# Second norm's rows and routed tiles' rows turned by transposing transfers, with a new written order

## The reference, cut to what matters

```python
# x: (8, 1024, 256)
h = layernorm(x) * (1 + ca) + sa
x = x + ga * attention(h)               # 16 heads, causal softmax
h = layernorm(x) * (1 + cb) + sb        # the second norm
shared = silu(h @ w1.T) * (h @ w2.T) @ w3.T          # hidden 1024
scores = sigmoid(h @ router_w.T)                     # 8 experts, the 2 best of scores + bias
routed = sum over the two chosen e of scores[e] * (silu(h @ a_e.T) * (h @ b_e.T)) @ w3_e.T
x = x + gb * (shared + routed)
```

## Time and profile before

| what | value |
|---|---|
| three timed runs | 2047.53, 2051.80, 2051.96 us; median 2051.8 us |
| the profiled execution, its own time | 2070.19 us |
| its span | 2068.4 us |
| granted TensorE clock, mean | 0.954 of full speed |
| batches 2 to 6 ("loop") | 199 us each, 422 to 1418 us of the span |
| "end" | from about 1594 us to 2068.4 us, 474 us |

### The profile page before, as it was taken

How to read it: one execution, slowest core, us unless ns; L and a number is a source line. 1 busy time by engine, 2 the same in 40 slices (tenths; PEclk the granted TensorE clock), 3 DMA queues, 4 the chain that set the end, 5 groups by cost and what they waited for, 6 DMA issues and landing times.

```text
span 2068.4 us, 48010 instructions
## 1 busy us (share of the span) xinstructions
PE 1855.7 (90%) x17942; PEld 1081.0 (52%) x17942; DVE 1589.9 (77%) x4447; ACT 1078.7 (52%) x1417; POOL 820.1 (40%) x825
## 2 busy tenths in 40 slices
PE   5688899998999899989998998999988998999884
PEld 2233445453545454545454544555444886888663
DVE  7998989888888888888888887988972565665573
ACT  1566646654665565556555565565545354444321
POOL 1021243424333333332343234323333377776452
PEclk7789999999999999999999999999999999999997
DMA  4347321102111111111111212021214366876794
GB/s 133 118 150 216 107 68 38 48 19 77 48 38 43 52 48 38 48 48 48 38 56 40 56 36 72 22 66 30 58 36 156 78 113 125 163 140 107 193 291 138
DMA packets 109664, 175.69 MB, mean 85 GB/s; under 512 B 14576, under 2 KB 80376, under 8 KB 108288
## 3 DMA queue, kind: packets, MB, share of 16 engines
q1 hardware_dynamic: 82656, 136.37, 22.0%
q0 software_dynamic: 26592, 36.00, 9.5%
q10 hardware_dynamic: 192, 0.26, 0.1%
HBM read 76.43 MB, written 70.44 MB: 71 GB/s over the span
## 4 chain that ended last, share of the span: by engine, by line
PE 58%; DVE 16%; DMA 8%; SPq 5%; ACT 5%; issue 4%; POOL 3%; another core or an unknown queue 1%; ACTq 0%; DVEq 0%; POOLq 0%
PE pair L1831 13%; PE pair L1816 10%; PE pair L1770 6%; PE pair L1794 6%; PE pair L1863 5%; PE pair L1883 5%; DVE pair L1264 4%; PE pair L1744 3%; ACT arena L1061 3%; DVE max_part L1258 2%; PE pair L1910 2%; PE pair L1874 2%; SPq L656 2%; DMA v_sb<-sum 2%; SPq L657 2%
## 5 line engine op out<-in xcount | busy, mean ns | idle before, releaser
L1061 ACT ACTIVATE arena<-pair 128x1024 f32<-128x1024 f32 (+1 forms) x640 | 574.9, 938 | 295.8 <-PE pair L1794 286.5
L1264 DVE CUSTOM_DVE_ANT_0 pair<-pair,mask 128x512 f32<-128x512 f32 (+3 forms) x1024 | 472.1, 520 | 51.6 <-PE pair L1770 48.5
L1831 PE MATMUL pair<-feat_parts,ffn_sb 128*128 128x512 f16 x1536 | 393.1, 391 | 3.6 <-ACT arena L1061 2.4
L875 POOL TENSOR_SCALAR_AFFINE_SELECT arena<-arena 128x512 f32<-128x512 f32 x256 | 163.5, 650 | 560.7 <-ACT arena L1061 560.1
L1816 PE MATMUL pair<-arena,v_sb 128*32 128x256 f32 (+1 forms) x5120 | 320.7, 369 | 6.7 <-issue 3.9
L1258 DVE TENSOR_REDUCE max_part<-pair 128x2 f32<-128x1024 f32 x256 | 312.5, 1221 | 14.3 <-PE pair L1770 10.9
L938 POOL DMA_INDIRECT sum<-arena,feat x142 | 229.8, 1618 | 103.4 <-DVE arena L1490 49.2
L1770 PE MATMUL pair<-arena 48*128 48x512 f16 (+3 forms) x1536 | 213.2, 341 | 54.9 <-ACT arena L1061 19.1
L944 POOL TENSOR_TENSOR hidden<-silu_h,hidden 128x512 f16<-128x512 f32 x128 | 152.2, 1193 | 238.1 <-ACT hidden L1094 237.8
L1794 PE MATMUL pair<-arena 50*128 50x256 f16 (+1 forms) x2560 | 215.4, 265 | 21.8 <-ACT arena L1061 6.2
L1831 PEld LDWEIGHTS pair<-feat_parts,ffn_sb 128*128 128x128 f16 x1536 | 136.5, 100 | 170.6 <-issue 47.0
(11 more groups left out here) (211 smaller groups left out, 2345.2 us busy)
## 6 DMA issues: line engine op xcount, KB each, us to landing
arena<-parts SPq DMA_DIRECT2D x380, 64.0 KB, 2.3
feat<-lists SPq DMA_DIRECT2D x71, 265.0 KB
sum<-feat_parts SPq DMA_DIRECT2D x9, 1024.0 KB, 8.3
rows<-x SPq DMA_DIRECT2D x8, 1024.0 KB, 5.5
x_sb<-x SPq DMA_DIRECT2D x16, 512.0 KB, 4.9
sum<-norm SPq DMA_DIRECT2D x14, 512.0 KB, 4.2
ffn_parts<-hidden SPq DMA_DIRECT2D x8, 768.0 KB, 4.4
arena<-ffn_parts SPq DMA_DIRECT2D x8, 768.0 KB, 7.4
```

The costliest lines, as they stand in the source:

```text
L875: gp.affine_select(p, p, [[0, GH], [1, P]], ALU.is_ge, 0.0, 0, -1).then_inc(masked, 1)
L1061: sc.activation(to[:, :, lo:QC], of[:, :, lo:QC], ACT.Exp, scale=SCALE / QK_SCALE ** 2).then_inc(exp_done, 1)
L1264: last = vec.tensor_tensor_reduce(scored, scored, mask[:, 512 - nk:], scale=1.0, scalar=NEG, op0=ALU.add, op1=ALU.max, accum_out=max_part[ ...
L1831: last = mm(to[:, 0:512], w_up[s][W_PART[i]][:, f, m * RH + h * P:m * RH + (h + 1) * P], feat_parts[:, A_PART[i], f, c * 512:(c + 1) * 512 ...
```

## The change

PE no longer turns the second norm's rows or the tiles' rows, and ACT and DVE no longer copy them. SP issues transposing transfers that write feat_parts and tile_feat directly. The steps `low:h` and PSUM banks for `ln` and `xr` are gone. tile_feat has four buffers in place of two. A tile now takes two transfers: a transposing one of 256 rows x 512 values from the list in memory, and a plain one of the last 9 f32 of each row. For a half of the second norm there are 4 transposing transfers, each of 128 rows x 512 values, SBUF to SBUF. All six lists and their banks are written anew.

```diff
+            def turn_rows(f, v, h):
+                sp.wait_ge(row_low, at_half(f, h))
+                if v == "second" and h == 0:
+                    sp.wait_ge(zeroed, ZEROED)
+                if past(f):
+                    sp.wait_ge(up_full, at_up(f - 1, 8 * h + 7))
+                    sp.wait_ge(router_full, at_half(f - 1, h))
+                for t in range(4 * h, 4 * h + 4):
+                    sp.dma_start_transpose(feat_parts[:, :, :, t * P:(t + 1) * P].rearrange("p a f n -> p (a f) n"),
+                                           rows16[:, t, 0:2 * D]).then_inc(feat_in[h], 16)
...
                 if i >= 2:
-                    sp.wait_ge(tile_turned, at_tile(i - 2))
                     sp.wait_ge(id_ready, at_tile(i - 2))
+                if i >= 4:
+                    sp.wait_ge(tile_full, at_tile(i - 4))
...
-                sp.dma_start(tile_rows[i % 2], list_rows(row)).then_inc(rows_in[i % 2], 16)
+                sp.dma_start_transpose(tile_feat[i % 4].rearrange("p a f n -> p (a f) n"),
+                                       list16[bass.ds(row, ROWS), 0:2 * D]).then_inc(tile_in_turn[i % 4], 16)
+                sp.dma_start(tile_rows[i % 2][:, :, D:], list_rows(row)[:, :, D:]).then_inc(rows_in[i % 2], 16)
...
-            def take_rows(i, of):
-                act.wait_ge(tile_turned, at_tile(i))
-                sc.activation(tile_feat[i % 2].rearrange("p a f n -> p (a f n)"), of[:, 0:4 * ROWS], ACT.Copy).then_inc(tile_taken, 1)
...
-            def feature_low(f, v, h):
...
-            def tile_turn(i, to):
...
             def tile_up(i, to):
-                pe.wait_ge(tile_taken, at_tile(i))
+                pe.wait_ge(tile_in_turn[i % 4], (i // 4 + 1) * 16)
...
                     elif kind == "router":
-                        pe.wait_ge(feat_high, at_half(f, h))
-                        pe.wait_ge(feat_low, at_half(f, h))
+                        pe.wait_ge(feat_in[h], (f + 1) * TURNED)
```

More of the change, by code:

```diff
@@ L126 @@
[L126 to L147, removed]
+        scores:4 scores:5 max:1:7 max:1:8 max:1:9 scores:6 values:0 values:1 values:2 share:0 share:1 raw:0 qk:2 turn_out:0 normalise:0 max:1:10 values:3
@@ L153 @@
[L153 to L164, removed]
@@ new lines @@
+        scores:14 values:10 values:11 halves:0 values:12 values:13 shifts:1 max_turn:1 scores:15 scores:16 max:2:0 values:14 values:15
+        scores:17 raw:2 max:2:1 values:16 ln:0 scores:18 max:2:2 turn_out:1 scores:19 normalise:1 scores:20 turn_out:2 normalise:2 max:2:3 values:17 values:18
+        scores:21 max:2:4 scores:22 router:0 up:0:0 up:0:1 load_x:1 route:0 scores:23 scores:24 up:0:2 values:19 up:0:3 raw:3 max:2:5 up:0:4 up:0:5
+        scores:25 scores:26 scores:27 rank:0 place:0 turn_out:3 normalise:3 values:20 values:21 max:2:6 raw:4 scatter:0 scatter:1 max:2:7
@@ L191 @@
-        scores:18 down:-2:0 down:-2:1 down:-2:2 max:2:0 scores:19 ln:0 low:0 down:-1:0 max:2:1 max:2:2 values:16 values:17 router:0 values:18 route:0
-        values:19 raw:3 scores:20 scores:21 up:0:0 up:0:1 turn_out:2 normalise:2 up:0:2 up:0:3 up:0:4 max:2:3
-        scores:22 up:0:5 turn_out:3 normalise:3 down:-1:1 down:-1:2 scores:23 max:2:4 max:2:5 rank:0 place:0 hid:0 values:20 values:21 raw:4 up:1:0
-        scores:24 up:1:1 up:1:2 up:1:3 up:1:4 up:1:5 scores:25 max:2:6 max:2:7 values:22 values:23 scatter:0
@@ L323 @@
 WORK["start"] += [("max", 0, p) for p in range(MAXES)] + [("max_turn", 0)]
-DOUBLE = ("scores", "max", "op", "ot", "ln", "turn", "qk", "v", "mods", "tup")
-SINGLE = ("down", "router", "max_turn", "rank", "count", "xr", "ty")
+DOUBLE = ("scores", "max", "op", "ot", "turn", "qk", "v", "mods", "tup")
+SINGLE = ("down", "router", "max_turn", "rank", "count", "ty")
 BANKS = 8
@@ L620, in adaln_layer @@
         SHIFTED = 16 * 2
+        TURNED = 16 * 4
         PADS_OUT = 16 * (NE + 1)
```

337 lines of the change are left out of this document (168 added, 169 removed).

## The result

The changed kernel takes 1963.49 us (median of 4 runs, 1959.63 to 1969.33) against 2049.66 us (2043.60 to 2051.96, 4 runs) for the kernel before: ratio 0.9586, 95% interval 0.9553 to 0.9619, 86 us less. The profiled execution took 1963.7 us, its span is 1961.8 us.

The account below looks back on a forecast made before the run. PE was taken to bound both the loop batches and "end"; 21 (tiles) + 12.6 (norm) + 22 (hole) - 3 ("second") = 53 us off the 2051.8 us median gave about 2000 us, range 1975 to 2070 us.

Parts of the forecast that it names:

- Part 1: Tiles: removing PE's turns, 71 x 0.45 = 32 us at full price, counted as 21 us saved.
- Part 3: Loop batches: new list moves load_x1 ahead, shrinking the hole at the x load; 22 us saved over five batches.
- the lists carried at nothing: All stages: the rest of the new lists, not priceable from the old trace, so no term in the sum.
- Part 2: Second norm: removing PE's turns of its rows saves 1.8 us a batch, 12.6 us over seven batches.
- the discounts to 80% and a quarter: Tiles: 53 before 1900 us counted at 80%, 19 us; the 18 behind at a quarter, 2 us.
- Part 4: Transposing transfers: 1.27 us a tile at the low end taken, 5.07 at the high; 17.4 ns per 256 B, issues 0.59 us.
- The 3 us lost in "second": Stage "second": only 3 to 4 us between ln:0 and router:0, so 3 us lost, once.
- Rival (a): New wait at router:0 or scores:20 from slower transfers, PE standing 21 us over seven batches; 2020 to 2025 us, 17%.
- (b): Loop batches: the hole at the x load stays because scatters cannot come earlier; about 2022 us, 12%.
- (c): Transfers become the bound of "end" at 5.07 us a tile, making the kernel slower; about 2190 us, 15%.
- one of its signs: In "end": DMA share of 0.9 or more, with PE waiting for the transposing transfer before a tile's first matmul.
- (d): Everywhere, "first" too: the newly written lists open holes and give the gain back; 2045 to 2060 us, 8%.

Follow-up runs that it names:

- before_spread_later: Kernel before with the loop list's first use of x (spread1:0, spread1:1) moved behind up:5:4; 2047.27 us, ratio 0.9984.
- after_again: The changed kernel itself, unchanged, run again beside variants of the kernel before with new lists; 1962.51 us, ratio 0.9569 to the kernel before.
- old_lists: The changed kernel's code with all written lists from the kernel before, without its low steps; 2154.65 us, ratio 1.0524.
- after: The changed kernel as first measured and profiled, nothing else altered; median 1963.49 us, ratio 0.9586 to the kernel before.
- before_again: The kernel before, unchanged, profiled once more; profiled execution 2046.3 us, span 2044.6 us.
- full_rows_2: Repeat of the changed kernel with a tile's plain load fetching whole 1060-byte rows instead of their last 36 B; 1965.98 us, ratio 0.9604.

## Why the prediction was wrong in size

The sign and the reason for it held: PE bound both stages, and work taken off it paid. The forecast of 53 us off was short of the 86 measured. Of the 32 us between the two spans' 84.9 and the sum's 52.6, Part 1 is 16, Part 3 with what else the loop's list does is 16, and the lists carried at nothing are 7; Part 2 takes 8 back, which is luck for the number. By the prediction's own steps:

- **Part 1** (21 us) measured 37, 2 of them the norm's. Its full price, 71 x 0.45 = 32 us, was right; the discounts to 80% and a quarter are the first step that failed: PE's turns came off the stretch whole.
- **Part 3** (22 us; its bounds 0 and 32) measured 38 us for the loops. Their idle time on PE fell by 24 us, near the 22 that were forecast; the other 14 are the same matmuls in less time, for which the clock is the cause that the rows show. That is the second step that failed: I had priced the hole by PE's standing time and left out that the clock is at 0.50 for 3 to 5 us behind it. Two things were wrong in the reasons: x's time is set by the scatters and not by the place of load_x1, and DVE's next late step has to move too, as `before_spread_later` shows.
- **"The rest of the new lists I cannot price from the old trace"**, carried at nothing, is the third, and smaller. It is "last" -13.6 us (its cause was not looked for), the tail -13.8, against "second" +9.8 and the tiles +10.9 by the list alone, which is -6.7 together. (The two profiles of before differ by 7 us in "second" and 10 in the tiles, so these terms are rough.) The tail's was in the diff: three ty steps behind up:15:5. The list of "end" decided whether Part 1 was worth 37 us or nothing.
- **Part 2** (12.6 us) measured 3 us in the five batches, which is within what executions differ by, and 2 us more up to the first tile. 1.3 us of PE a batch came off (1.8 forecast), but PE now waits for the features, 8.9 + 6.6 us in all, with 5.5 us for shifts. With turns on PE it waited about as long for the turned rows' copies and for the steps before them, so these waits don't settle it. What holds a batch at 191 us when PE is relieved stays open.
- **Part 4**: a tile's transfers were put at 0.25 us more than before. The DMA time in the stretch went from 0.71 x 417.1 = 296 us to 0.94 x 380.1 = 357 us, 0.86 us a tile (which has two norm halves in it). From the q1 rows, (0.289 x 1961.8 - 0.225 x 2000.2) x 16 us, plus the 18176 row packets of 63.6 ns that went, less as many small ones at 9.6 ns, over 105472 packets of 256 B gives 27 ns; the packets of that size in the trace of `after_again` have a mean of 25.0 ns and a median of 18, and 17.4 was forecast. The low end was the right kind, at one and a half times its price. SP's time for an issue was wrong, too, 1.27 us in place of 0.59; `old_lists` shows what that costs where the list leaves no room for it. The 3 us lost in "second" did not come from the transfers (186.3 and 186.4 us).
- **Rival (a)** was right in its mechanism: with the old lists it is the main loss (79.6 us of PE waits). In the changed kernel it is 15.5 us of short waits. **(b)** is out: the scatters could come earlier. **(c)** is out, though the DMA share of 0.94 was one of its signs: a tile passes every 380.1 / 71 = 5.4 us, while its DMA time is 1.9 us ((1024 x 27 + 256 x 9.6) / 16 ns), and no wait of PE for a tile's transposing transfer is among the changed kernel's. The estimate worked out from the Trainium skill, "VectorE: DVE Perf Modes", "The three transpose paths", 10.5 us a tile, does not agree with that, nor does its 390 ns for TensorE: eight blocks took 0.45 us. The Trainium skill, "Advanced Engine Details and Errata", section "X-Bar Transpose (TRN2)", says that transposing DMAs are as fast as regular ones; here a byte took 27 / 256 = 0.105 ns against 63.6 / 1060 = 0.060 ns, so by packet time a byte took 1.8 times as long. **(d)** shows in the changed kernel in "second" (+10 us) alone.

Put together from the table: 37.0 (tiles, Part 1) + 4.9 (Part 2: 2.8 in the loops, 2.1 before the first tile) + 38.0 (loops, Part 3 and what else their list does) + 6.7 (unpriced lists) - 1.7 (batches 0 and 1, but for what the list does to "second") = 84.9 us, the difference of the two spans.

## What to carry to other kernels

When a change comes with a new order of the work, price the order as a part of its own: read where each list leaves work for the end, and what the queues that issue in order have in front of the new transfers. Then test the order without the change, and the change without the order; here one is worth 44 us (25 in another group of runs), the other costs 108, and together they give 85. A hole in a busy TensorE is worth its length and the slow clock behind it: in the loops here 24 us of idle time went, and 14 us of busy time with them.

## What the runs showed of the hardware

- A transposing transfer's issue holds SP 1.26 to 1.27 us (medians of `after`), whether it turns 128 x 512 values SBUF to SBUF or 256 x 512 from memory; of the plain ones beside it a tile's small load takes 0.43 and a stack transfer 0.59 us. The last of four lands within 1.4 us of the end of its issue.
- Its packets are of 256 B (105472 of them in `after_again`), 25 to 27 ns each in traffic.
- TensorE's granted clock fell to 0.50 (1.2 GHz) while PE stood for 6.4 and for 9.85 us, and was full again 3 to 5 us after work came back (`before_again`, `old_lists`).
- The DMA share of a stretch can be over 1 (1.06 in `full_rows_2`), so a share of 0.94 is no proof of a bound.
- Groups of runs differ by 1% on the same kernel (2046.6 to 2069.2 us), and in the gain of a change by half a per cent and more (0.9569 and 0.9631 for the changed kernel, with one chip number; 0.9789 and 0.9874 for the lists alone). A comparison of variants by less than that needs one group.
